# Cross network of a recommender tower: layer 1 in 19 passes per tile, one DMA for a chunk's rows, and other queues for the prologue's transfers

## The reference, cut to what matters

```python
x0 = xk = e
for W in (f0, f1, f2):                      # (39*39,128), (128*39,128), (128*39,128)
    z = einsum('bfd,bgd->bfgd', x0, xk).reshape(b, f*g, d)
    xk = einsum('bpd,pm->bmd', z, W);  outs.append(xk)
h = concatenate([sum(concatenate(outs, 1), -1), dense_ctx], 1)      # (512, 400)
y = relu(relu(h @ W_top1 + b_top1) @ W_top2 + b_top2) @ W_top3
```

## Time and profile before

| | us |
|---|---|
| median of 3 runs | 685.78 (683.43 to 687.0) |
| the profiled execution | 684.99 |
| its span in the profile | 683.0 |
| first layer 2 matmul | 48.48 |
| end of the last tile's layer 2 | about 658 |

### The profile page before, as it was taken

How to read it: one execution, slowest core, us unless ns; L and a number is a source line. 1 busy time by engine, 2 the same in 40 slices (tenths; PEclk the granted TensorE clock), 3 DMA queues, 4 the chain that set the end, 5 groups by cost and what they waited for, 6 DMA issues and landing times.

```text
span 683.0 us, 11480 instructions
## 1 busy us (share of the span) xinstructions
PE 642.6 (94%) x2942; PEld 510.8 (75%) x2942; DVE 564.9 (83%) x1914; ACT 383.4 (56%) x1157; POOL 532.2 (78%) x528
## 2 busy tenths in 40 slices
PE   3279999999999999999999999999999999999998
PEld 1156777767768787888868787888878888888867
DVE  4459897988989897989879897989879797988760
ACT  0447574746657574747467474746557474655431
POOL 6756989898999899897879989897959988574420
PEclk9989999999999999999999999999999999999998
DMA  9536533104040404013130404004040221200000
GB/s 185 92 93 232 151 74 92 30 8 116 10 116 8 116 9 116 6 26 98 31 94 6 116 9 110 13 8 115 7 115 7 63 62 36 82 1 1 1 1 0
DMA packets 70979, 41.92 MB, mean 61 GB/s; under 512 B 45889, under 2 KB 55761, under 8 KB 70786
## 3 DMA queue, kind: packets, MB, share of 16 engines
q1 hardware_dynamic: 58286, 35.53, 19.5%
q10 hardware_dynamic: 7380, 4.38, 3.1%
q0 software_dynamic: 5248, 1.29, 1.9%
HBM read 39.20 MB, written 1.94 MB: 60 GB/s over the span
## 4 chain that ended last, share of the span: by engine, by line
PE 73%; DVE 12%; issue 7%; POOL 3%; SPq 2%; ACT 2%; DMA 1%; DVEq 0%; POOLq 0%
PE y L853 18%; PE y L855 16%; PE y L854 16%; DVE scaled L756 10%; PE late L871 4%; PE side L860 4%; PE acc L835 3%; PE acc L829 3%; PE acc L830 3%; PE y L871 2%; ACT scaled L560 1%; PE late L882 1%; SPq L376 1%; POOL z_parts L463 1%; DVE z L717 1%
## 5 line engine op out<-in xcount | busy, mean ns | idle before, releaser
L756 DVE SCALAR_TENSOR_TENSOR scaled<-y,x_rows,scaled 128x128 f32<-128x128 f32 x1728 | 466.4, 343 | 71.2 <-ACT scaled L560 41.9
L560 ACT ACTIVATE scaled<-y,x_rows 128x128 f32<-128x128 f32 x768 | 218.3, 366 | 216.2 <-PE y L855 200.7
L853 PE MATMUL y<-w_hi,x_parts 128*128 128x512 f32 (+1 forms) x640 | 276.8, 432 | 6.8 <-DVE scaled L756 3.2
L855 PE MATMUL y<-w_hi,x_parts 128*128 128x512 f32 (+1 forms) x640 | 248.1, 388 | 0.0
L854 PE MATMUL y<-w_lo,x_parts 128*128 128x512 f32 (+1 forms) x640 | 247.4, 387 | 0.0
L463 POOL TENSOR_TENSOR z_parts<-z,z_parts 117x512 fp32r<-117x512 f32 (+1 forms) x107 | 138.4, 1294 | 33.4 <-ACT z_parts L514 32.5
L452 POOL DMA_INDIRECT emb_quads<-in_small_tables_dram,quad_rows x144 | 138.8, 964 | 27.2 <-issue 15.3
L853 PEld LDWEIGHTS y<-w_hi,x_parts 128*128 128x128 f32 x640 | 120.5, 188 | 44.7 <-DVE scaled L756 19.3
L855 PEld LDWEIGHTS y<-w_hi,x_parts 128*128 128x128 f32 x640 | 120.1, 188 | 25.0
L854 PEld LDWEIGHTS y<-w_lo,x_parts 128*128 128x128 f32 x640 | 121.0, 189 | 18.2
L478 POOL TENSOR_TENSOR sum<-sum,scaled 128x512 f32<-128x512 f32 x63 | 81.6, 1295 | 29.1 <-DVE scaled L756 28.3
(11 more groups left out here) (95 smaller groups left out, 360.2 us busy)
## 6 DMA issues: line engine op xcount, KB each, us to landing
z<-x_turned SPq DMA_DIRECT2D x311, 78.0 KB
x_three<-x_turned SPq DMA_DIRECT2D x48, 78.0 KB
x_turned<-emb_quads SPq DMA_DIRECT2D x156, 8.0 KB
w_sb<-in_w_dram SPq DMA_DIRECT2D x1, 2496.0 KB
emb_quads<-in_small_tables_dram,quad_rows POOLq DMA_INDIRECT x144
s_sb<-in_w_dram ACTq DMA_DIRECT2D x12, 160.0 KB
x_turned<-emb_singles SPq DMA_DIRECT2D x89, 2.0 KB
x_turned<-emb_quads SPq DMA_DIRECT2D x64, 2.0 KB
```

The lines of the kernel that those rows point to most:

```text
L560: done = act.activation(scaled[:, k % 2, BY_ACT.index(j), i * M:(i + 1) * M], y2[n % RING][:, i * M:(i + 1) * M], ACT.Copy, scale=x0_rows[ ...
L756: dve.scalar_tensor_tensor(part, y2[n % RING][:, i * M:(i + 1) * M], x0_f, part, ALU.mult, ALU.add).then_inc(terms_in, 1)
L853: pe.matmul(dst, x1_hi[:, t % 2, cols], hi, start=True, stop=False)
L855: pe.matmul(dst, x1_lo[:, t % 2, cols], hi, start=False, stop=True).then_inc(y_ready, 1)
```

## The change

**Layer 1 in 19 passes.** The 780 pairs are dealt anew over seven chunks. Six chunks still hold three shifts each (shifts 0 to 17, 117 rows). Shifts 18 and 19 are 78 pairs; 44 of them fill the eleven free rows of chunks 0 to 3, which now have 128 rows. The 34 pairs left stand three times in the last chunk (102 rows): one copy meets high x high, one high filter x low, one low filter x high, so one matmul does what took three. The copies are told apart by a column of ones and zeros (`third_sb`): the high part is the product rounded where the column is one and zero elsewhere, and the low part, product minus high part, is the rest; the filter is treated alike. The last product has its own second operand, `x0_rest`, in SBUF.

**DMAs.** A chunk's rows come in one DMA of 117 rows (partition 3f + r) instead of three of 39. The eleven extra rows of four chunks are one DMA (`more_rows`, after chunk 3; the product of chunk 0 waits for it), the last chunk takes eight (`rest_rows`). `x0_three` takes two instead of three, `x0_stack` four instead of three.

**Prologue.** W1's loads go from ScalarE's queue to the head of SyncE's. W0's two arrays come in nine DMAs each instead of one each, and their free rows are cleared by VectorE first. Of tile 0's stores SyncE keeps 13, ScalarE has the others. ScalarE also issues `x0_three`, chunks 0, 2 and 4 and the extra rows of tile 0; SyncE chunks 1, 3, 5 and the last. W1's high part is made by VectorE instead of ScalarE, and the dense part of the tower moves between ScalarE's high parts. `small_rows` and `y_sb` lie in other buffers to make room.

```diff
+FULL = 3 * F
+MORE = P - FULL
+MORE_CHUNKS = 4
+MORE_SHIFT = 18
+REST = ((11, 18, 10), (32, 18, 7), (11, 19, 9), (31, 19, 8))
+REST_PAIRS = sum(n for _, _, n in REST)
...
 def depth(c):
-    return F * turns(c)
+    if c == C0 - 1:
+        return 3 * REST_PAIRS
+    return P if c < MORE_CHUNKS else FULL
...
         def turned_rows(queue, u, c):
-            for r in range(turns(c)):
-                shift = 3 * c + r
-                queue.dma_start(z[F * r:F * r + F, c, :], x0_dram[u, shift:shift + F, :]).then_inc(a_in[c], 16)
+            x = x0_dram[u, 3 * c:3 * c + F, :]
+            queue.dma_start(z[0:FULL, c, :], bass.AP(x.tensor, x.offset, [[COLS, F], [COLS, 3], [1, COLS]])).then_inc(a_in[c], 16)
+        def more_rows(queue, u):
+            x = x0_dram[u, MORE_SHIFT:MORE_SHIFT + MORE, :]
+            queue.dma_start(z[FULL:P, 0:MORE_CHUNKS, :],
+                            bass.AP(x.tensor, x.offset, [[COLS, MORE], [COLS, MORE_CHUNKS], [1, COLS]])).then_inc(more_in, 16)
+        def rest_rows(queue, u):
+            for at, f, shift, n in rest_places():
+                queue.dma_start(x0_rest[at:at + 3 * n, :], thrice(x0_dram[u, f:f + n, :])).then_inc(a_in[C0 - 1], 16)
+                queue.dma_start(z[at:at + 3 * n, C0 - 1, :], thrice(x0_dram[u, f + shift:f + shift + n, :])).then_inc(a_in[C0 - 1], 16)
...
+            for j in range(W1_PIECES):
+                load_filter(sp, j)
+            store_singles(sp, 0, (0,))
+            for i in (8, 4, 7, 0, 5):
+                store_quad(sp, 0, i, (0,))
...
+                for c in (1, 3, 5, 6) if u == 0 else range(C0):
...
+                    if c < C0 - 1:
+                        turned_rows(sp, u, c)
+                    else:
+                        rest_rows(sp, u)
                     if c == 2 and u > 0:
-                        three_blocks(u)
+                        blocks_of(u)
+                    if c == MORE_CHUNKS - 1 and u > 0:
+                        more_rows(sp, u)
...
             def high_part(u, c):
-                copy(z_hi[0:k, n % Z_RING, :], z[0:k, c, :]).then_inc(z_hi_in, 1)
+                if c == C0 - 1:
+                    done = act.activation(z_hi[0:k, n % Z_RING, :], z[0:k, c, :], ACT.Copy, scale=third_sb[0:k, 1:2])
+                else:
+                    done = copy(z_hi[0:k, n % Z_RING, :], z[0:k, c, :])
...
+            first_filter(act, w0a_raw, w0a)
+            first_filter(act, w0b_raw, w0b)
...
+            store_singles(act, 0, (1,))
+            store_singles(act, 1, (0, 1))
+            for i, copies in ((4, (1,)), (0, (1,)), (1, (0, 1)), (2, (0, 1)), (3, (0, 1)), (6, (0,))):
+                store_quad(act, 0, i, copies)
+            act.wait_ge(stored[0], 16 * STORES)
+            three(act, 0)
+            turned_rows(act, 0, 0)
+            more_rows(act, 0)
+            turned_rows(act, 0, 2)
+            turned_rows(act, 0, 4)
+            three_to_psum(0)
...
             def product(u, c):
                 if c == 0:
                     dve.wait_ge(three_up, u + 1)
+                    dve.wait_ge(more_in, 16 * (u + 1))
...
+                other = x0_rest if c == C0 - 1 else three_ps
+                dve.tensor_tensor(z[0:k, c, :], z[0:k, c, :], other[0:k, :], ALU.mult).then_inc(prod, 1)
...
+            def second_filter_parts(i):
+                dve.wait_ge(w1_in[i], 64)
+                dve.tensor_copy(w1_hi[:, i:F:4, :], w1_raw[:, i:F:4, :]).then_inc(w1_hi_in, 1)
...
             def contract(u, c):
-                pe.wait_ge(z_hi_in, n + 1)
-                pe.matmul(acc0[:, :], w0_hi[0:k, c, :], z_hi[0:k, s, :], start=c == 0, stop=False)
-                pe.matmul(acc0[:, :], w0_lo[0:k, c, :], z_hi[0:k, s, :], start=False, stop=False)
+                last = c == C0 - 1
+                if not last:
+                    pe.wait_ge(z_hi_in, n + 1)
+                    pe.matmul(acc0[:, :], w0_hi[0:k, c, :], z_hi[0:k, s, :], start=c == 0, stop=False)
+                    pe.matmul(acc0[:, :], w0_lo[0:k, c, :], z_hi[0:k, s, :], start=False, stop=False)
...
+                weights = w0_lo if last else w0_hi
+                pe.matmul(acc0[:, :], weights[0:k, c, :], z_lo[0:k, s, :], start=False, stop=last).then_inc(z_done, 1)
```

138 lines of the change are left out of this document (73 added, 65 removed).

## The result

| | before | after |
|---|---|---|
| median, us | 686.39 (683.43 to 687.0) | 703.45 (702.42 to 707.51) |
| profiled execution, span | 683.0 | 705.5 |
| layer 2 of tile 2 starts from | 122.5 | 133.6 |
| the next 13 tiles | 498.9 | 511.6 |
| the end behind them | 61.6 | 60.3 |

The change makes the kernel slower: 1.0268 times the time of before, with a 95% interval of 1.0243 to 1.0294. Forecast were 674 us and a range of 669 to 681.

The account below looks back on a forecast made before the run. TensorE was taken to bound tiles with layer 3, a ring of GpSimd, TensorE, ScalarE and VectorE the others. 684.99 - 7.0 (matmuls) + 0.6 (last product) - 5.4 (prologue) = 673.2, with 0.8 for the median 674.0 us; range 669 to 681.

Parts of the forecast that it names:

- The matmuls, -7.0: Chunk 6, on the path in both kinds of tile: two matmuls fewer save 0.467 us in each of 15 tiles.
- rival B: Loop: the matmuls were covered by GpSimd, so only the prologue's gain and some 1 us stay; about 679, chance 0.13.
- Those 13.9 us hide it: Loop loads: chunk 0's product can wait for the extra rows (4.6 us into the loads, 2.6 landing) at no cost.
- The last product, +0.6: Loop: both operands in SBUF cost the product nothing, GpSimd beside it 0.15 us in four tiles; bounds 0 to 4.
- T = 26.3: Prologue: tile 0's stores have all landed at 26.3 us instead of 28.2, set by ScalarE's issues.
- From T to the first product, 4.5: Prologue: two DMA issues of 1.8 us and 2.6 to land put the first product at 30.8, against 33.40.
- From the product to layer 2: Prologue: 7.9 us of products and low parts, 1.9 to layer 2 and 1.5 added put layer 2 at 42.1.
- Tile 1's first product: After the prologue: its extra rows land at 50.6 for a product at 56.0 before, the prologue's gain of 5.4 us.
- VectorE's W1 pairs: Prologue: four copies at 1.28 us with their subtractions take 10.7 us, to 30.4, hidden just barely by the loads.
- Rival A: Prologue: the queues give nothing since SyncE's slow pace belongs to the time until about 35 us; 680, chance 0.19.
- Rival C: Prologue: a backlog in SyncE's queue, W1 at its head, keeps 1.4 us per issue; slower, 695, chance 0.08.

Follow-up runs that it names:

- e3: The kernel before without the first two of chunk 6's three passes (part of layer 1 left out): 677.32 us, ratio 0.9874.
- e6: e5 with W1's loads, W1's high part and the stores back where the kernel before had them: 683.42 us, ratio 0.9989.
- e10: e6 with `x0_rest` copied by ScalarE into `x0_three`'s PSUM bank, so that the last product reads PSUM: 678.87 us, ratio 0.9932.
- e1: The changed kernel with the extra rows' load moved ahead of all chunks' loads: 688.58 us, ratio 1.0048.
- e5: e1 with W0 laid out on the host, two loads for eighteen and nothing to clear: 683.90 us, ratio 1.0012.
- e2: The changed kernel with the last product reading `three_ps` in PSUM (wrong rows for the last chunk): 703.15 us, ratio 1.0271.
- e4: The kernel before with the last product reading `x0_three` in SBUF instead of its PSUM copy: 688.23 us, ratio 1.0051.
- e11: The changed kernel with W0 laid out on the host and nothing else: 702.80 us, ratio 1.0261.
- e12: e10 with SyncE issuing chunk 0 and the extra rows first in tile 0, ScalarE taking chunk 5: 680.50 us, ratio 0.9942.
- e7: The kernel before with one DMA per chunk's rows, shift outermost in its pattern (`x0_three` too): 718.18 us, ratio 1.0494.
- e13: The kernel before with x0's fourth block transposed from 117 rows of `x0_three` instead of 39: 680.63 us, ratio 0.9934.
- e9: The kernel before with one DMA per chunk's rows, field outermost, 117 rows in the last chunk, matching filters and the 117-row transposition: 678.96 us, ratio 0.9924.

## Why the prediction was wrong, point by point

In the tiles the excess over the kernel before adds up from single edits. In the 13 tiles: 19 passes -5.7 (e3), the operand in SBUF +2.8 (e6 to e10), the late rows +15.9 (e1 to after), together +13.0 against 12.7 measured. On the way to tile 2: W0's pieces +5.1 (e1 to e5), the queues +0.4 (e5 to e6), the late rows +3.6 (e1 to after), the rest +2.0 (before to e6). These four are steps of one chain of kernels, so their sum of 11.1 proves nothing; each comes from two single executions and is sure to some 2 us only (e2 and the changed kernel differ by 1.8 there).

- **The matmuls, -7.0: right.** 0.44 us a tile measured for 0.467, with and without layer 3 (e3: 37.85 us for 38.26 and 37.60 for 38.04, forecast 37.8 and 37.6); rival B fell. In the changed kernel the last product took most of it back in some tiles.
- **"Those 13.9 us hide it": the step that failed, and it carries the sign.** Two things were wrong in it. The 13.9 us of one tile were taken for all of them. In the trace of before the time from `x0_three`'s issue to the product is 16 to 18 us in four of the fifteen tiles, 13.2 to 13.9 in four, and in seven under 10: 7.0, 7.7, 7.8, 9.9, 9.9, 8.7 and 9.7. Two rows of before show one of these seven, 7.7 us:

```profile
80.10 1.14 SPq L401 DMA_DIRECT2D x_three<-x_turned  x3
...
87.79 0.68 DVE L717 TENSOR_TENSOR z<-z,three_ps 117x512 f32<-117x512 f32 x1
```

  And the extra rows were to be issued within 4.6 us of the first load, at 0.42 us for each of eleven issues. That was the price of a DMA of 39 rows. One of 117 rows takes 0.84, so that the extra rows are issued by 7.4 us (168.03 to 175.39), and the product starts at 10.2, 2.9 us later (forecast 2.6). Exactly the seven tiles with under 10 us became 10.2 to 11.0. The forecast put the cost at nothing; the waits of 13.3 us, and the half clock behind them, made it 15.9 us in the 13 tiles and about 15 by the medians (after to e1). By the forecast's own price the sum would have been 4.6 + 2.6 = 7.2 us, still early enough in all but tile 1, which the forecast had treated by itself: the list of slacks and the price of the issue were needed both. That a wait can cost TensorE its clock as well was in no term.
- **The last product, +0.6: the size was off.** The row it rests on the earlier trace rows is a subtraction with both operands in SBUF from the prologue, 687 ns, taken as proof that the product would not be longer. It took 1.07 us on average in the loop, where GpSimd is at work on SBUF beside it, and seven of the 13 tiles became 0.3 us longer, not four in all. Measured: 3.5 us (e4), inside the bounds of 0 to 4.
- **The stores, T = 26.3: wrong by 6.7** (32.97). The eighteen pieces of W0 were priced at 0.47 us each, the price of other loads; they took 0.71 on average, the eight that bring a few rows three times 0.79, the wide ones 1.69 and 0.85. The landing was put at 2.6 us; the identity, issued at 15.40 and part of the same wait, landed 7.4 us later, while SyncE's queue moved W1. So it can matter which queue carries W1. With W0 laid out on the host the identity is issued at 3.4 to 3.6 in all runs. With W1 in the other queue it landed at 9.7 and 12.8 (e5, e11), and VectorE waited 0.7 and 4.3 us for it; with W1 behind it in the same queue it was there when VectorE came, at 9.7 and 8.6 (e6, e10). None of these is near 2.6 us after the issue. The sum of W0 was to be done at 15 to 16 and was done at 24.1. ScalarE's stores ended at 32.6 instead of 23.7; the 2.6 us of landing behind them were only 0.4. SyncE's own stores ended at 31.1, so ScalarE's queue alone could not have brought T far down.
- **From T to the first product, 4.5: wrong by 3.9.** The product started at 41.34, 8.4 us behind T, after VectorE had waited 4.47 us for the rows of chunk 0 and the extra ones. With these two issued first it was 6.7 from the first load on (e12). From the product to layer 2 it was 11.6 us for 11.3, as forecast. Tile 1's first product, forecast at 50.6 and at 55.95 before, stood at 63.0: the prologue lost 7 us instead of gaining 5.4.
- **VectorE's W1 pairs** ended at 36.9 instead of 30.4, since they started 8 us late; each pair was shorter than assumed, the copy 0.81 us for 1.28:

```profile
27.87 0.81 DVE L844 CAST w_hi<-s_sb 128x1280 fp32r<-128x1280 f32 x1
28.72 1.49 DVE L846 TENSOR_TENSOR w_lo<-s_sb,w_hi 128x1280 fp32r<-128x1280 f32 x1
```

  By the section "Mode 2×_2P — use both read ports for one tensor" of the Trainium skill's page "VectorE: DVE Perf Modes" the prediction had worked out about 0.7, an estimate; the measurement is nearer to it than to the 1.28 the sum used, and outside the bounds of 1.1 to 1.45 taken from rows.
- **Rival A** (the queues give nothing) had the outcome of the queues right: taking W1 and the stores back changed 0.2%, within the interval (e5 to e6). Its sign came in part: SyncE issued eight stores in 11.23 us, 1.4 each, from 19.90 to 31.1, but its loads from 32.85 on at 0.9 each.
- **Rival C** forecast 695, slower, by a mechanism in the same queue, but another one: a slow pace of SyncE past 45 us. From 44 us on the queue issued tile 1's stores at 0.47 us each in e1 (17 in 7.97), and likewise in the others but e7. The pace of 12 stores from 15.1 us on varied with the execution, in kernels that are alike up to there: 13.3 us in before, 11.4 in e13, 9.3 in e9. What sets it was not tried.

## What to carry to other kernels

A load that is moved back in its queue has to be checked against the smallest slack of all its repetitions, not against one of them; here 13.9 us stood in the row that was read and 7.0 to 9.9 in seven of fifteen tiles. The price of an issue belongs to a shape: 0.4 us for 39 rows does not hold for 117. A wait that makes TensorE idle can be charged twice, once as itself and once by the clock: look at the granted clock behind each wait before pricing it. And a result that needs one late load (the identity behind eighteen pieces) waits for the whole queue in front of it and for what other queues move meanwhile. Small loads that others wait for may be better first; e5 had the identity early, but only together with the pieces gone, and the order alone was not tried.
